# An expert loop with two TensorE signals per expert instead of four, its matmuls put in another order within a step

## The reference, cut to what matters

```python
# x: (1088, 256) normed rows; E = 64 experts, K = 6 chosen, CAP = 128 places each, I = 176
prob = softmax(x @ gate_w.T)                 # (1088, 64)
chosen = top_k(prob + gate_b, 6)
for e in range(64):                          # every expert takes its tokens, at most 128
    t = tokens_of[e]
    hidden = silu(x[t] @ w1[e].T) * (x[t] @ w3[e].T)      # 128 x 176
    y[t] += prob[t, e] * (hidden @ w2[e].T)               # 128 x 256
y += (silu(x @ ws1.T) * (x @ ws3.T)) @ ws2.T              # shared expert, 352 wide
out = h + y
```

## Time and profile before

| | us |
|---|---|
| median of 3 runs (lowest, highest) | 616.24 (614.47, 617.27) |
| the profiled execution: its own time | 620.34 |
| its span | 618.3 |
| the first product of expert 0 starts | 394.41 |
| the last indirect write (expert 59) starts | 588.87 |

### The profile page before, as it was taken

How to read it: one execution, slowest core, us unless ns; L and a number is a source line. 1 busy time by engine, 2 the same in 40 slices (tenths; PEclk the granted TensorE clock), 3 DMA queues, 4 the chain that set the end, 5 groups by cost and what they waited for, 6 DMA issues and landing times.

```text
span 618.3 us, 11166 instructions
## 1 busy us (share of the span) xinstructions
PE 515.4 (83%) x3894; PEld 406.9 (66%) x3894; DVE 432.1 (70%) x989; ACT 336.9 (54%) x798; POOL 223.5 (36%) x232
## 2 busy tenths in 40 slices
PE   3979952357646999999999989998998898889996
PEld 2757841123324999999988888676765675656785
DVE  5988998999997377667762247665655665645776
ACT  1587625355447677777752472455644555455630
POOL 2110002023322722222225123766666676556700
PEclk9996977586775999999999999999899899798999
DMA  8990000019000010000000101266665666566676
GB/s 265 381 328 0 1 0 0 1 47 288 21 1 0 28 28 28 27 28 28 2 3 1 51 22 28 64 173 184 200 183 153 196 183 187 158 179 176 199 289 230
DMA packets 43899, 67.40 MB, mean 109 GB/s; under 512 B 11022, under 2 KB 27015, under 8 KB 43716
## 3 DMA queue, kind: packets, MB, share of 16 engines
q1 hardware_dynamic: 36868, 64.62, 33.4%
q0 software_dynamic: 6976, 2.07, 1.6%
HBM read 66.81 MB, written 17.20 MB: 136 GB/s over the span
## 4 chain that ended last, share of the span: by engine, by line
PE 53%; DVE 23%; ACT 6%; issue 6%; DMA 4%; another core or an unknown queue 4%; SPq 1%; POOL 1%; ACTq 0%; DVEq 0%; POOLq 0%
PE ps L1116 9%; PE ps L745 7%; PE ps L743 6%; PE ps L744 6%; PE ps L963 5%; PE ps L750 4%; DMA region<-y_rows 3%; PE ps L921 2%; PE ps L1124 2%; PE ps L953 2%; DVE region L1748 2%; PE ps L1106 2%; DVE region L1804 2%; DVE region L1759 1%
## 5 line engine op out<-in xcount | busy, mean ns | idle before, releaser
L1116 PE MATMUL ps<-region 128*128 128x352 f32 x256 | 94.1, 493 | 4.6 <-ACT region L1453 3.3
L703 POOL DMA_INDIRECT y_rows<-region x60 | 63.2, 1053 | 50.9 <-ACT region L1445 31.0
L694 POOL DMA_INDIRECT region<-x_rows,region x64 | 68.5, 1070 | 20.2 <-issue 17.4
L743 PE MATMUL ps<-nTh,high 128*128 128x272 f32 (+2 forms) x248 | 74.3, 300 | 0.4 <-ACT region L1380 0.4
L744 PE MATMUL ps<-nTl,high 128*128 128x272 f32 (+2 forms) x248 | 71.8, 289 | 0.0
L1468 ACT ACTIVATE high<-region 88x512 fp32r<-88x512 f32 x64 | 40.4, 631 | 39.8 <-PE ps L745 20.1
L1116 PEld LDWEIGHTS ps<-region 128*128 128x128 f32 x256 | 45.8, 199 | 22.9 <-ACT region L1453 5.3
L1952 DVE SCALAR_TENSOR_TENSOR region<-region,ps 128x176 f32<-128x176 f32 x64 | 25.3, 396 | 50.8 <-issue 24.5
L1804 DVE TENSOR_TENSOR region<-ps,region 32x136 f32<-32x136 f32 x128 | 38.0, 297 | 31.5 <-PE ps L921 29.8
L653 POOL COPY region<-region 32x544 f32<-32x544 f32 x32 | 26.5, 827 | 89.5 <-DVE region L1823 88.0
L745 PE MATMUL ps<-nTh,pairs_low 128*128 128x272 f32 x192 | 55.6, 289 | 0.0
(11 more groups left out here) (265 smaller groups left out, 1355.8 us busy)
## 6 DMA issues: line engine op xcount, KB each, us to landing
region<-moe_w SPq DMA_DIRECT2D x64, 352.0 KB
region<-moe_w SPq DMA_DIRECT2D x64, 176.0 KB
y_rows<-zrow SPq DMA_DIRECT2D x1, 6528.0 KB, 26.0
region<-y_rows SPq DMA_DIRECT2D x8, 768.0 KB, 10.2
region<-wqkv SPq DMA_DIRECT2D x8, 384.0 KB, 3.2
region<-ffn_w SPq DMA_DIRECT2D x2, 1024.0 KB, 8.0
region<-patches SPq DMA_DIRECT2D x3, 384.0 KB, 8.3
region<-patches SPq DMA_DIRECT2D x1, 1152.0 KB, 10.7
```

The costliest lines, as they stand in the source:

```text
L694: nc.gpsimd.indirect_dma_start(out=xb[m8], out_offset=None, in_=x_rows, in_offset=bass.IndirectOffsetOnAxis(ap=sloti[:, at:at + 1], axis=0 ...
L703: nc.gpsimd.indirect_dma_start(out=y_rows, out_offset=bass.IndirectOffsetOnAxis(ap=sld[m8], axis=0), in_=yb[m], in_offset=None, bounds_che ...
L743: nc.tensor.matmul(out, parts_a[0], parts_b[0], start=first, stop=False)
L1116: mm = nc.tensor.matmul(ps[:, 2 + m % 2, 0:2 * EI], xbT[m % 2][:, c, :], w13[m][:, c, :], start=(c == 0), stop=(c == DC - 1))
```

## The change

- TensorE increments one semaphore, `s_step`, at the last matmul of a step, and `s_eh13` after the first product; `s_xtb`, `s_ehtr` and `s_y` are gone. `tokens_turned`, `hidden_turned` and `rows_made` say which count of `s_step` stands for what.
- The order in a step is now: first product of n, transposes of the hidden rows of n-1, second product of n-2, the table's matmul, transposes of the tokens of n+2 (before: n+1, at the head of the step).
- Transposed hidden rows use two PSUM banks (`HT_BANK`) in turn, transposed tokens one.
- The table's work is spread over steps 2, 4, 6 (matmuls), 3, 5, 7 (masks, largest values) and 0 and 1 of the next block; it has no signal of its own inside the loop. The shared expert's tiles 6 to 8 go to steps 0 and 1.
- GpSimd does `put` before `gather` in a step; `gather` waits for much less. ScalarE's order becomes Silu, `w2` rounding, hidden copy, token copy, row copy.
- `late_sums` of tile 1 moves behind the loop, beside tile 4.

```diff
+def tokens_turned(e):
+    return e + 1
+def hidden_turned(e):
+    return e + 4
+def rows_made(e):
+    return e + 5
...
-        EARLY = (0, 1, 2, 3, 5)
+        EARLY = (0, 2, 3, 5)
+        HT_BANK = (4, 1)
...
             def load2(e, m):
-                need(sp, s_y, e - 3)
+                sp.wait_ge(s_step, rows_made(e - 4))
...
-                pool.wait_ge(s_tab, b + 1)
-                need(pool, s_xtb, e - 7)
-                need(pool, s_sld, e - 7)
-                need(pool, s_got[m], 4 * (e - 4 - m) + 16)
+                if m8 == 0:
+                    pool.wait_ge(s_tab, b + 1)
+                if e < EB:
+                    need(pool, s_got[m], 4 * (e - 4 - m) + 16)
...
             def pool_step(n, b, m8):
+                if 0 <= n - 3 < E - LATE:
+                    put(n - 3, (m8 - 3) % EB)
                 if 5 <= n + 5 < E:
                     gather(n + 5, b + (m8 + 5) // EB, (m8 + 5) % EB)
-                if 0 <= n - 3 < E - LATE:
-                    put(n - 3, (m8 - 3) % EB)
...
+            def turn_hidden(e, k):
+                pe.wait_ge(s_eh, e + 1)
+                need(pe, s_ehl, e - 1)
+                for c in range(2):
+                    mm = nc.tensor.transpose(ps[0:EH, HT_BANK[k % 2], c * P:(c + 1) * P], eh[k % 2][:, c * EH:(c + 1) * EH],
+                                             ident[:, :])
+                return mm
...
             def pe_step(n, b, m8):
-                if 0 <= n + 1 < E:
...
-                    mm.then_inc(s_xtb, 1)
...
                     mm.then_inc(s_eh13, 1)
...
-                    mm.then_inc(s_ehtr, 1)
...
-                    mm.then_inc(s_y, 1)
...
+                if n == 0:
+                    pe.wait_ge(s_hsh, 3 * CH)
+                    pe.wait_ge(s_slot, 2)
+                    shared_rows(6, 5)
+                    shared_rows(7, 6)
+                if 0 <= n - 1 < E - 1:
+                    last = turn_hidden(n - 1, (m - 1) % 4)
+                if n == 1:
+                    shared_rows(8, 7)
+                if 0 <= n - 2 < E:
+                    last = second_product(n - 2, (m - 2) % 4)
...
+                if m8 in (2, 4, 6) and 0 <= n < E - 2 * EB:
...
+                    spread_groups(6, q, c)
+                if m8 == 0 and EB <= n < E - EB:
+                    place_slots(b + 1)
+                if 0 <= n + 2 < E:
+                    e = n + 2
+                    pe.wait_ge(s_got[e % 4], 4 * (e - e % 4) + 16)
+                    need(pe, s_xbT, e)
+                    for c in range(DC):
+                        last = nc.tensor.transpose(ps[:, 0, c * P:(c + 1) * P], xb[e % EB][:, c * P:(c + 1) * P],
+                                                   ident[:, :])
+                if last is not None:
+                    last.then_inc(s_step, 1)
...
+                if 0 <= n - 1 < E:
+                    e, k = n - 1, (m - 1) % 4
+                    act.wait_ge(s_w2[k], 4 * (e - k) + 16)
+                    if e >= 2:
+                        act.wait_ge(s_step, rows_made(e - 2))
+                    nc.scalar.activation(w2_h[k % 2], w2[k], ACT.Copy).then_inc(s_w2h, 1)
+                    act.wait_ge(s_step, hidden_turned(e))
+                    nc.scalar.activation(ehT_h[k % 2], ps[0:EH, HT_BANK[k % 2], 0:2 * P].rearrange("p (c n) -> p c n", c=2),
+                                         ACT.Copy).then_inc(s_ehT, 1)
...
+                if m8 == 1 and EB <= n < E - EB:
+                    keep_slots(b + 1)
+                if m8 in (3, 5, 7) and 0 <= n < E - 2 * EB:
...
+                    mask_groups(ps[:, 6, 0:w], a, w)
+                    if c == 2:
+                        best_slots(b + 2)
+                        widen_slots(b + 2)
```

More of the change, by code:

```diff
@@ L416, in build @@
         s_xbz = sem("s_xbz")
-        s_xtb = sem("s_xtb")
+        s_step = sem("s_step")
         s_xbT = sem("s_xbT")
@@ L1054, in spread_groups @@
                 src = spread_e[:, e0:e0 + EB, :] if isinstance(q, int) else spread_e[:, bass.ds(e0, EB), :]
-                nc.tensor.matmul(ps[:, bank, 0:w], src.rearrange("p e g -> p (e g)"), group[:, a:a + w],
-                                 start=True, stop=True).then_inc(s_rep, 1)
+                return nc.tensor.matmul(ps[:, bank, 0:w], src.rearrange("p e g -> p (e g)"), group[:, a:a + w],
+                                        start=True, stop=True)
             def place_slots(q):
                 pe.wait_ge(s_wide, q + 1)
-                nc.tensor.matmul(ps[:, 6, 0:EB], wide8.rearrange("p g j -> p (g j)"), lay8[:, 0:EB],
-                                 start=True, stop=True).then_inc(s_tabps, 1)
+                return nc.tensor.matmul(ps[:, 6, 0:EB], wide8.rearrange("p g j -> p (g j)"), lay8[:, 0:EB],
+                                        start=True, stop=True)
             pe.wait_ge(s_xbz, 12)
@@ L1066, in _ @@
             for c in range(3):
-                spread_groups(5 + c, 0, c)
+                spread_groups(5 + c, 0, c).then_inc(s_rep, 1)
             shared(8)
             shared(9)
-            place_slots(0)
+            place_slots(0).then_inc(s_tabps, 1)
             second_shared(4, 3)
@@ L1073, in _ @@
             for c in range(3):
-                spread_groups(5 + c, 1, c)
+                spread_groups(5 + c, 1, c).then_inc(s_rep, 1)
             second_shared(5, 4)
             shared(10)
-            place_slots(1)
+            place_slots(1).then_inc(s_tabps, 1)
             shared(11)
@@ L1096, in row_sums, with second_product @@
                 mm.then_inc(s_sum, 1)
+            def turn_hidden(e, k):
[4 more added lines that the diff above has]
+                                             ident[:, :])
+                return mm
+            def second_product(e, k):
+                pe.wait_ge(s_ehl, e + 1)
+                pe.wait_ge(s_w2l, 2 * (e + 1))
+                need(pe, s_yb, e - 1)
+                if e < 2:
+                    pe.wait_ge(s_h4, 7 + 2 * e)
+                if e - 1 > E - LATE:
+                    pe.wait_ge(s_late, e - 1 - (E - LATE) + LATE)
+                for c in range(2):
+                    mm = product(ps[:, 5 + 2 * (k % 2), 0:D], (ehT_h[k % 2][:, c, :], ehT_l[k % 2][:, c, :]),
+                                 (w2_h[k % 2][:, c, :], w2_l[k][:, c, :]), c == 0, c == 1)
+                return mm
             def pe_step(n, b, m8):
                 m = m8 % 4
[L1101 to L1108 removed]
+                last = None
                 if n == 0:
@@ L1159, in _ @@
             pe.wait_ge(s_h4, NT)
-            for j in range(2):
-                late_sums(4, j, True)
+            for t in (1, 4):
+                for j in range(2):
+                    late_sums(t, j, True)
             pe.wait_ge(s_late, LATE + 3)
@@ L1855, in shared_sum @@
                 r = slice(0, rows(t))
-                dve.wait_ge(s_z, t + 1)
+                if t < 6:
+                    dve.wait_ge(s_z, t + 1)
                 V.tensor_tensor(h[r, t, :], ps[r, bank, 0:D], h[r, t, :], ALU.add).then_inc(s_h4, 1)
```

145 lines of the change are left out of this document (49 added, 96 removed).

## The result

| | before | changed |
|---|---|---|
| median (lowest, highest), us | 616.13 (614.47, 617.27), 4 runs | 625.4 (624.21, 627.71), 4 runs |
| ratio, 95% interval | | 1.0127 (1.0088 to 1.0167) |
| profiled execution, span, us | 620.34, 618.3 | 624.21, 622.5 |
| first product to last indirect write, us | 194.46 | 593.87 - 392.68 = 201.2 |

The account below looks back on a forecast made before the run. Prediction: TensorE bounds the kernel, its loop slowed by limited signal pace. Work 164.6 + 7.6 + 5.4 = 177.6 us in place of 194.46, -16.9, so median 599 us; range 587 to 612.

Parts of the forecast that it names:

- Signals: TensorE's signals in the MoE loop: 2.1 per step in place of 4.4 removes idle time and half clock, -29.9 us.
- rival B: TensorE's signal pace is tied to GpSimd's indirect DMAs, two signals per pair: gain 7.5, so 608.5 us; chance 0.20.
- rival C: The number of TensorE's signals isn't the cause and the same stops come: 616 us, 613.2 to 619; chance 0.09.
- One signal at the step's end: Hidden rows' signal now waits for second product and tokens; slack 0.24 us per step, remaining lateness costs +7.6 us.
- Rival D: Slower: everything hangs on the late step-end signal; stretch 62 x (L + 2.10) + 24.9, L its lateness; chance 0.09.
- The table: TensorE waits 0.9 us at `place_slots` for VectorE's mask and largest values in each of 6 blocks: +5.4 us.
- Order of matmuls: TensorE's same matmuls in another order in the loop: 0, the work stays at 164.6 us.
- the work: TensorE's loop stretch of 194.5 us less 29.9 of idle time and half clock: 164.6 us, unchanged.
- GpSimd, 0: 119 indirect DMAs take 162 us, below TensorE's sum; later gathers and dropped waits in the loop change nothing: 0.
- Gathers land late and TensorE waits for them at L1182: Named way for the prediction to fail: TensorE waits at its token transposes for late gathers; no size given.
- Shared tiles: The shared expert's matmuls, moved to the first steps: the same 24 records or so, 0 us.

Follow-up runs that it names:

- i1: Changed kernel with 8 more increments per step on a semaphore nobody awaits, 10.1 signals per step: 625.62 us, where before took 615.4.
- i2: Kernel before with 8 more increments per step on a semaphore nobody awaits, 12.4 signals per step: 618.65 us, where before took 615.4.
- i3: Kernel before with only the first 8 gathers and no indirect writes: 581.35 us, where before took 615.4.
- e2: Kernel before with only the first 8 gathers and no indirect writes: 579.19 us, where before took 588.2.
- e1: Changed kernel with only the first 8 gathers and no indirect writes: 588.02 us, where before took 588.2.
- g3: Changed kernel with only the first 8 gathers and no indirect writes, in a later series: 584.7 us, where before took 587.5.
- f1: Kernel before, run again unchanged: 588.06 us, where its series gives before 587.3.
- f2: Changed kernel, run again unchanged: 592.21 us, ratio 1.0064 to before, which took 587.3.
- h3: Kernel before with GpSimd issuing the write of expert n-3 ahead of the gather of expert n+5: 590.55 us, ratio 1.0038.
- g1: Changed kernel with the gather ahead of the write again and two of its waits given back: 592.65 us, ratio 1.0109 to before.
- h1: Changed kernel with gathers ahead of the write and further ahead, 7 steps at first, later 6, in place of 5: 592.62 us, ratio 1.0061 to before.
- h4: Kernel before with gathers seven steps ahead in place of five: 586.04 us, ratio 0.9969.

## Why the prediction was wrong

**The term that failed is "Signals", -29.9 us.** It said that TensorE gets its signals out at a limited pace, that 4.4 per step exceed it and 2.1 do not. The reading of the trace up to there was right: the signal is late, not the work. That the queue is made by the number was argued, from a mean interval of 0.7 us that was nothing but 283 signals over 194.5 us, and no row showed two signals spacing each other; so "that they leave one by one agrees", said there of the Trainium skill's page, wasn't shown by the trace either. i1 and i2 refute the queue: with 10.1 and 12.4 signals per step the waits stay as they were, and TensorE keeps losing its time. The rows held the other suspect too, GpSimd's indirect DMAs running wherever signals were late; it was in the text as rival B, but only as a pace for the signals, with its price a gain. i3 shows that without them there is no lateness: 34.0 us less than before in its series, of which the same cut gives 9.0 in the 588 condition too (e2).

**Where the time is, in the 616 condition.** Clean steps and the rest, with the clean length from i3 and e2 (before), and from e1 and g3 (changed; in the 588 condition only, though before's is the same in both):

| | steps | clean | the rest: stops and half clock |
|---|---|---|---|
| before | 194.9 | 158.7 | 36.2 |
| before, 12.4 signals (i2) | 194.2 | 158.7 | 35.5 |
| changed | 201.9 | 163.8 | 38.1 |
| changed, 10.1 signals (i1) | 200.4 | 163.8 | 36.6 |

The changed kernel is 7.0 us longer there: 5.1 by its order, 1.9 by stops, and the last is little more than what each kernel differs by from its twin with extra signals, 0.7 and 1.5. (In the 588 condition the rest is 3.6 us for before and 5.0 for the changed kernel, f1 and f2.) So the change took nothing from the stops and added the order's cost. It is rival C, "the number of signals isn't the cause and the same stops come", with an added price that C lacked; C's 616 was 9 us too low.

**One signal at the step's end, +7.6.** The slack of 0.24 us was rightly seen: TensorE's stops now are at L757, where it said. As a size it was meant for what is left of the lateness after a cure. The mean lateness of this signal is 0.6 us. Rival D's formula gives 62 x (0.6 + 2.10) + 24.9 = 192 for the stretch; measured are 201.2. A mean doesn't tell the cost of lateness that comes in pieces of 2.9 us between steps that are on time.

**The table, +5.4.** Right, as far as the step lengths tell: 0.66 us of wait per block in place of 0.9 and a step 0.76 longer, 4.6 us in six blocks; the waits at L1079 in the first trace are 3.3 us in four records.

**Order of matmuls, 0, and the work, 164.6.** The work of before is 158.7, not 164.6: a busy TensorE was taken for clean work, but matmuls around the stops are longer too: 4.3 us more busy time than in i3 in the steps at full clock alone. What i3 takes away is 36 us, not 29.9. The price of the order, apart from the table, is 5.1 - 4.6 = 0.5 us, near the 0 that was said.

**GpSimd, 0.** Too low in the 588 condition; in the other it can't be told from the stops. The working had 162 us for its 119 DMAs and noted that this is not far below TensorE's sum; with clean steps of 158.7 it lies above, and GpSimd comes to bound the loop as well (f2 has no pause in it, and h3's write-first order costs before 2.6 us). "Gathers land late and TensorE waits for them at L1182" was named as a way to fail: 3.4 us in f2. The dropped waits of `gather` brought nothing, since the write ahead of it in the queue waits longer, 7.7 us.

**Shared tiles, 0.** The matmuls cost the same. But in steps 0 and 1 they stretch these to 4.0 and 3.2 us (before 1.9 and 2.1) and hold up the rows of expert 0, and with them GpSimd: its first write starts 10.3 us after the first product in f2 and 6.2 in f1.

## What to carry to other kernels

When a signal is late, its number is one suspect among several, and it can be tested without a new loop: add increments that nobody awaits. The kernel before with nearly three times its signals and no longer steps (i2) would have stopped this change before it was written. And take the length of a loop's clean steps from a run without the disturber (here without GpSimd's indirect DMAs), not from busy time in a disturbed trace; an order that is 5 us longer shows there at once, and so does an engine that lies just below the bound.

## What the runs showed of the hardware

- In the 616 condition TensorE's signals come up to 2.9 us late (3.3 in i1) with GpSimd's indirect DMAs about, while ScalarE's to VectorE, in the same microseconds, take 0.04. Without the indirect DMAs none is late (i3, one run). It comes and goes between executions far apart: the same kernel takes 616 or 588 us, with 36.2 or 3.6 us over its clean steps.
- The number of TensorE's signals, 2.1 to 12.4 per step of 2.34 us, changed neither their lateness nor, within 1.5 us, the length of the 63 steps (in single runs).
- An indirect DMA occupies GpSimd for 1.05 to 1.07 us on the mean, and 0.30 us pass before the next even where it waits for nothing. 119 of them are 162 us. Two orders of them were tried on the changed kernel and gave no time (g1, h1); starting gathers earlier made before 1.9 us faster (h4, 12 runs against 28), by a way that isn't shown.
